# Another order of TensorE's and ScalarE's calls in the first half of a two-stage transformer kernel

## The reference

```
q, k, v = out @ Wq + bq, out @ Wk + bk, out @ Wv + bv       # 16 heads of 16
Qf, Kf  = favor(q), favor(k)      # exp(u - h), exp(-u - h), u = xs @ omega, h = 0.5 sum(xs*xs)
S_t     = S_(t-1) + Kf_t (x) v_t ;  z_t = z_(t-1) + Kf_t    # causal, per head
a_t     = (Qf_t . S_t) / (Qf_t . z_t + 1e-6)
h       = layer_norm(out + a @ Wo + bo)
out     = layer_norm(h + relu(h @ W1 + bf1) @ W2 + bf2)     # W1 256 x 1024
```

## Time and profile before

| | us |
|---|---|
| median of three runs | 2773.57 (2766.88 to 2775.44) |
| the profiled execution | 2769.28 |
| its span | 2767.5 |
| TensorE busy | 2633.1 (95%) |
| VectorE busy | 2308.6 (83%) |
| ScalarE busy | 1513.2 (55%) |
| GpSimd busy | 1455.6 (53%) |
| matmuls of key sums, rounds 0 to 23: first and last start | 48.6, 1334.8 |

### The profile page before, as it was taken

One profiled execution on the slowest core, in us unless ns is written; L12 is line 12 of the kernel. 1 busy time (PEld: TensorE's weight loads), 2 busy tenths in 40 slices (PEclk: granted clock), 3 DMA queues, 4 the chain that ended last, 5 costly groups with the idle time before them and its releaser, 6 DMA issues.

```text
span 2767.5 us, 61567 instructions
## 1 busy us (share of the span) xinstructions
PE 2633.1 (95%) x21416; PEld 2152.8 (78%) x21416; DVE 2308.6 (83%) x5242; ACT 1513.2 (55%) x3109; POOL 1455.6 (53%) x1406
## 2 busy tenths in 40 slices
PE   7799999999999999999888899999999999999997
PEld 4588887888788878777676688888878778788876
DVE  5788888888888898988898888888888888888875
ACT  3454455445544554444335766767766666666661
POOL 2343344344433444444466766665666666776653
PEclk8999999999999999999999999999999999999999
DMA  3100000010000010000111100000110100101001
GB/s 101 28 9 9 17 2 16 9 38 2 1 1 13 11 39 9 17 17 24 45 48 45 32 10 17 14 17 14 32 29 24 36 16 29 32 29 32 17 26 43
DMA packets 77731, 65.63 MB, mean 24 GB/s; under 512 B 15394, under 2 KB 72698, under 8 KB 77434
## 3 DMA queue, kind: packets, MB, share of 16 engines
q1 hardware_dynamic: 77434, 61.70, 7.5%
HBM read 49.10 MB, written 12.58 MB: 22 GB/s over the span
## 4 chain that ended last, share of the span: by engine, by line
PE 72%; DVE 11%; issue 7%; POOL 6%; ACT 2%; DMA 1%; SPq 0%; DVEq 0%; ACTq 0%; POOLq 0%
PE PS L273 64%; PE PS L813 3%; DVE Z L1532 2%; DVE U L1678 2%; POOL ZC L2356 1%; PE PS L766 1%; PE PS L775 1%; POOL RL L2316 1%; POOL X0L L2320 1%; PE PS L486 1%; PE PS L424 1%; PE PS L843 1%; DVE X L1532 1%; DVE PX L1532 1%; DVE PS L1915 1%
## 5 line engine op out<-in xcount | busy, mean ns | idle before, releaser
L1335 ACT ACTIVATE PR<-PS,SM 128x256 f32<-128x256 f32 (+1 forms) x512 | 279.2, 554 | 103.4 <-DVE SM L1920 101.8
L1133 ACT ACTIVATE FB<-PS,BC 128x512 f32<-128x512 f32 x192 | 132.1, 688 | 347.2 <-PE PS L273 344.0
L1678 DVE TENSOR_TENSOR U<-PS,CST 128x512 f32<-128x512 f32 x384 | 236.7, 677 | 33.5 <-PE PS L273 33.4
L1915 DVE CUSTOM_DVE_ANT_0 PS<-PS,MSK 128x256 f32<-128x256 f32 (+1 forms) x512 | 202.6, 436 | 48.8 <-PE PS L273 47.5
L2316 POOL TENSOR_TENSOR RL<-FB,RH 128x512 fp32r<-128x512 f32 x96 | 131.6, 1371 | 204.3 <-DVE RH L1656 204.3
L2328 POOL TENSOR_TENSOR SBD<-SBD,TMP 128x256 f32<-128x256 f32 x84 | 65.2, 776 | 317.6 <-DVE TMP L1670 317.6
L273 PE MATMUL PS<-W2H,RH 128*128 128x256 f32 x768 | 227.6, 296 | 0.3 <-DVE RL L1659 0.3
L2451 POOL TENSOR_TENSOR SM<-SM,COL 128x8 f32<-128x8 f32 x128 | 215.2, 1682 | 10.6
L273 PE MATMUL PS<-W2H,RL 128*128 128x256 f32 x768 | 215.8, 281 | 0.0
L273 PE MATMUL PS<-W2L,RH 128*128 128x256 f32 x768 | 215.7, 281 | 0.0
L273 PE MATMUL PS<-X1H,W1H 128*128 128x512 f32 x384 | 159.3, 415 | 8.5 <-ACT FB L1133 6.6
(11 more groups left out here) (264 smaller groups left out, 8914.1 us busy)
## 6 DMA issues: line engine op xcount, KB each, us to landing
PX<-in_L_attn_x SPq DMA_DIRECT2D x16, 512.0 KB, 4.0
TB<-in_k_rot SPq DMA_DIRECT2D x64, 128.0 KB, 2.1
SG<-in_L_attn_W SPq DMA_DIRECT2D x24, 256.0 KB, 2.8
xp_scratch<-PX SPq DMA_DIRECT2D x8, 512.0 KB, 3.0
xs_scratch<-X SPq DMA_DIRECT2D x64, 64.0 KB, 1.5
ZS<-xs_scratch SPq DMA_DIRECT2D x16, 256.0 KB, 2.9
GG<-xp_scratch SPq DMA_DIRECT2D x7, 512.0 KB, 3.7
out<-GG SPq DMA_DIRECT2D x7, 512.0 KB, 4.2
```

The lines of the kernel that those rows point to most:

```text
L1133: e.activation(FB[:, hb % 2, :], PS[:, 5, :], ACT.Relu, bias=BC[:, l % 2, 4 + hb:5 + hb]).then_inc(*a_re.up(n, hb))
L1335: t = e.activation(PR[:, par, 256 * i + lo:256 * i + hi], PS[:, 3 + par, 256 * i + lo:256 * i + hi], ACT.Exp, bias=S[:, 40 + 2 * g + i:41 ...
L1678: e.tensor_tensor(heads(U[:, u % 6, :], 4), heads(PS[:, g, :], 4), bcast(CM, 4), ALU.mult).then_inc(*d_mk.up(n, u))
L1915: t = e.tensor_tensor_reduce(o, o, MSK[:, z:z + hi - lo], 1.0, NEG, ALU.add, ALU.max, S[:, 32 + 2 * g + i:33 + 2 * g + i])
```

## The change

TensorE's list of rounds 2 to 23: `up(m, 2)` goes from behind `proj(n, 0)` to behind `down(m, 0)`; `values(n, 0)` stands in front of `down(m, 0)` and `values(n, 1)` behind `down(m, 1)`; `scores(n, 0)` goes in front of `key_sums(n)`; `up(m, 6)` in front of `down(m, 3)`; `down(m, 4)` in front of `up(m, 7)`; `down(m, 6)` in front of `turn_x(n + 1)`. ScalarE's list: both `attention` casts and `relu(m, 2)` in front of the features, `relu(m, 3)` behind all of them, `numerators(n, 1)` in front of `relu(m, 7)`, `numerators(n, 2)` behind `high_row`. In the second half ScalarE's waits for the end of the first half and for the bias transfers stand in front of the first `gelu` (tile 8) instead of at tiles 4 and 8. VectorE's, GpSimd's and SyncE's lists stay.

```diff
@@ tensor, for n in range(2, 24)
             up(m, 1)
             proj(n, 0)
-            up(m, 2)
             proj(n, 1)
             proj(n, 2)
             proj(n, 3)
+            values(n, 0)
             down(m, 0)
-            values(n, 0)
+            up(m, 2)
+            down(m, 1)
             values(n, 1)
-            down(m, 1)
             favor(n, 0, 2)
...
             up(m, 4)
+            scores(n, 0)
             key_sums(n)
-            scores(n, 0)
             down(m, 2)
             up(m, 5)
             sums(n, 0)
             scores(n, 1)
+            up(m, 6)
             down(m, 3)
-            up(m, 6)
             sums(n, 1)
             scores(n, 2)
+            down(m, 4)
             up(m, 7)
-            down(m, 4)
             sums(n, 2)
             scores(n, 3)
             down(m, 5)
             turn_h(w)
+            down(m, 6)
             if n < 23: turn_x(n + 1)
-            down(m, 6)
             if n < 23: up(w, 0)
@@ scalar, for n in range(2, 24)
             attention(w, 0)
+            attention(w, 1)
+            relu(m, 2)
             features(n, 0, 2)
-            relu(m, 2)
-            attention(w, 1)
             features(n, 1, 3)
             features(n, 2, 0)
+            features(n, 3, 1)
             relu(m, 3)
-            features(n, 3, 1)
             keep_rows(n, 0)
...
             relu(m, 6)
+            numerators(n, 1)
             relu(m, 7)
-            numerators(n, 1)
             high_mid(w, 0)
             high_mid(w, 1)
-            numerators(n, 2)
             if n < 23: high_row(n + 1, 0)
             if n < 23: high_row(n + 1, 1)
+            numerators(n, 2)
@@ scalar, gelu(q, hb)
             e.wait_ge(*f_ga[hb].at(q))
+            if q == 0 and hb == 0:
+                e.wait_ge(*t_bf.at(7))
+                first_half_over(e)
@@ scalar, second half's loop
-            if u == 4:
-                e.wait_ge(*t_bf.at(7))
...
-            if u == 8:
-                first_half_over(e)
```

## The result

| | before | after |
|---|---|---|
| median, runs | 2769.85 (2764.32 to 2775.44), 10 | 2778.83 (2775.85 to 2785.81), 10 |
| profiled execution, span | 2769.28, 2767.5 | 2784.48, 2782.7 |
| TensorE, VectorE busy | 2633.1, 2308.6 | 2641.6, 2305.7 |

The ratio is 1.0035, with a 95% interval of 1.0023 to 1.0048: 9.7 us slower (6.4 to 13.3). The forecast was +9.1. As a time, 2782.5, it lies 3.7 above the measured median: it was laid on 2773.57, the median of three runs of the kernel before, where ten runs give 2769.85.

The account below looks back on a forecast made before the run. TensorE, busy 977 of 990 us, was taken as the bound, its waits being all there is to win. Terms +5.0 + 0.6 + 1.0 + 2.5 made +9.1 us on the median 2773.57, stated as 2782.5; eight-in-ten range 2769 to 2792.

Parts of the forecast that it names:

- Scores and key sums: Late relu 3 makes VectorE's block 3 cast meet GpSimd's RL, delaying the scores: +0.28 in 18 rounds, 0.6 in round 20.
- The upper bound of +1.5: Worst case per round for scores and key sums, if VectorE's subtraction lets both ZC products go first.
- TensorE's edit alone: Scores in front of key sums with nothing to wait for would let down begin 0.22 earlier per round.
- Masks: Later VectorE chain makes sums(n, 0) wait some 0.2 for masks where a batch half begins (five rounds): +1.0.
- The split of the turns: down(m, 6) between turn_h and turn_x costs 0.12 for one more change of kind in 21 rounds: +2.5.
- Its later end moves high_row and lower. Covered: turn_x's later end moves high_row and lower(n + 1) by 1.0 to 1.4, without cost to TensorE.
- attention(w, 1) is early, so attn_out gets slack: ScalarE's second attention cast comes earlier, giving attn_out slack; listed among the edits at nothing.
- Rival 1: Ports are no obstacle: cast and subtraction end at 757.7, add_wo in time; -1.0, 2772.5 us; chance 0.28.
- Rival 2: The 1.0 behind the masks in sums(n, 2) goes if VectorE does norm1_b earlier; 2754 us; chance 0.06.
- Rival 3: Subtraction waits for both ZC products, or delayed chain misses sums(n, 1): +1.25 in 19 rounds, 2806 us; chance 0.10.

Follow-up runs that it names:

- e1: Changed kernel with relu(m, 3) put back in front of features(n, 3) on ScalarE; measured +4.1 us against the kernel before.
- e5: Changed kernel with GpSimd's RL of block 2 and ZC products cut to 16 of 512 columns; -1.1 us against the kernel before.
- e8: Kernel before with relu(m, 3) behind features(n, 3) and GpSimd's block 2 RL and ZC products on 16 of 512 columns; -5.0 us against before.
- e3: Kernel before with only relu(m, 3) moved behind features(n, 3) on ScalarE; +23.0 us against the kernel before.
- e2: Kernel before with only scores(n, 0) moved in front of key_sums(n) on TensorE; -1.4 us against the kernel before.
- e4: Changed kernel with down(m, 6) behind turn_x(n + 1) again, so the turns stand together; +17.7 us against the kernel before.
- c1: Changed kernel run a second time, unedited; +14.1 us against the kernel before, ratio 1.0051.
- e7: Kernel before with ScalarE's whole features part ordered as in the changed kernel, TensorE's order kept; +8.9 us against the kernel before.
- g1: Kernel before with scores(n, 0) in front of key_sums(n) and masks(n, 2) in front of norm1_b(w); -22.1 us against the kernel before.
- e6: Changed kernel with masks(n, 2) in front of norm1_b(w) on VectorE; -5.5 us against the kernel before.

## Why the prediction came out right, and where it did not

- **Scores and key sums, +0.28 in 18 rounds and 0.6 in round 20: right.** Cast 0.7 (0.58), subtraction 1.67 (1.65), wait 0.4 to 0.5 (9.6 in 19), pair +0.31. e1, e5 and e8 show the cause. Over rounds 2 to 20 the pair costs 5.3 in either trace of the changed kernel, where 5.6 was forecast. I had overlooked rounds 10 and 18, in which the key sums waited 0.6 for ZC before; there the pair became 0.1 to 0.2 shorter. And the 0.6 of round 20 came in the first trace alone. It all hung on a reckoning that put the cast 0.45 inside RL; it was 0.29. e3 shows how thin that is: RL 0.2 earlier and relu 3 0.3 later against `up(m, 4)`, and the price is 1.0. The upper bound of +1.5 was no fancy. I then wrote e3's expectation without redoing that reckoning, and missed by 15 us or more.
- **TensorE's edit alone, -0.22: right** (e2: 760.35 - 758.38, where the last matmul of `up` starts, makes 1.97 for the 2.24 of before: -0.27).
- **Masks, +1.0: too small (0.34 in five rounds, 1.7), cause incomplete.** I put it on add_wo's lateness. e1 and e2 have add_wo early and the same 0.34: the normaliser waits for the key sums behind the scores. e3 has the key sums first and add_wo late, and loses there too. In the changed kernel both come within 0.1 of each other, so either alone is enough.
- **The split of the turns, +2.5: mis-sized.** The prediction took 0.12 for one more change of kind. turn_x's group lasts 794.88 - 794.08 = 0.80, against 0.79; turn_h's 0.82 with `down` behind it, where 783.10 - 782.20 made 0.90. Together they are no longer than before (1.62 and 1.69), so the term is 0 in place of 2.5.
- **"Its later end moves high_row and lower. Covered": failed.** In rounds 3, 5 and 6 VectorE has the prologue's or the weights' work behind `lower`, so state(n, 3), numerators(n, 3) and relu(m, 0) come late. Round 5, ScalarE after:
```profile
296.44 0.38 ACT L1141 COPY NUM<-PS 128x256 f32<-128x256 f32 x1 [3.62 <-DVE TMP L1669]
```
  `up(3, 1)` starts at 297.55, 0.45 behind a matmul whose neighbours stand 0.12 apart. With 0.25 in rounds 10 and 18 it makes 1.8, and e4 gets that back. I followed round 13 and transferred it.
- **"attention(w, 1) is early, so attn_out gets slack": not free.** VP of round 20 is waited for 1.0 more. VectorE before, and after:
```profile
1135.94 4.57 DVE L1532 SCALAR_TENSOR_TENSOR PX<-Z,ST,PX 128x256 f32<-128x256 f32 x4
```
```profile
1147.85 5.58 DVE L1531 SCALAR_TENSOR_TENSOR PX<-Z,ST,PX 128x256 f32<-128x256 f32 x4
```
  GpSimd after, in that time:
```profile
1147.43 2.90 POOL L2310 TENSOR_TENSOR X<-X,BB 128x512 f32<-128x512 f32 x2
1150.35 2.80 POOL L2319 TENSOR_TENSOR X0L<-NUM,X0H 128x512 fp32r<-128x512 f32 x2
```
  Before, the second X0L product started at 1140.50, behind the norm; the earlier cast of ScalarE brought it inside. A fourth tile met a product: 1.0. The runs bear it out: every kernel with that cast early (changed, c1, e1, e4 to e7) waits 2.86 to 2.88 there, and before, e2, e3, e8 and g1 wait 1.85 to 1.87.
- **The clock: a cost that the prediction didn't name.** Behind the waits for VP TensorE ran at half clock for longer than before (last section): 2.8 us more in the first trace, which costs 1.4, and 2.1 more in c1, which costs 1.0.
- **The sum.** Of the pair's 5.3 the stretch, which starts at the key sums of round 2, holds 5.0. 5.0 + 1.7 + 0 + 1.8 + 1.0 + 1.4 = 10.9, near the stretch's +11.8; for c1 it is 10.5 of 11.2. The forecast of 9.1 was low by two or three, and as near as that by luck: the split's 2.5, which weren't there, stood for some 5 us that it left out.

Rival 1 would have been right without the overlap (e5: -1.1 for its -1.0). Rival 2's place was real and its condition as stated: the 1.0 in sums(n, 2) went only when VectorE's order changed (e6). Rival 3 didn't come in the changed kernel. e3 came nearest to it: there the cast itself fell into a ZC product.

What stays open: what makes the 12 us spread ahead of round 2; why the medians of e1, e3 and e4 stand 3.5 to 7 above their stretches (for e3 the short wait in front of round 23 may be 4 of it); and the 0.7 to 0.9 that the sum leaves.

## What to carry to other kernels

Before an activation or a cast is moved, write down which instruction of GpSimd runs when VectorE's next cast, or its next instruction with two SBUF operands, is asked for, in every kind of round and not in one. Here a late input cost little by itself; one that fell into a product cost the product's rest, and the next instruction one product more. And look for norms or other long groups in front of what a stalled matmul waits for: swapping two lines there was worth more (15.6 in the stretch) than this change cost.

## What the runs showed of the hardware

- When both engines have work queued, they take turns, one instruction each: a subtraction of 0.69 takes 1.65, a norm tile of 0.47 takes 1.4, and GpSimd's products grow only from 1.3 to 1.4 or 1.5. A cast of 0.42 takes up to 1.33.
- A wait can cost more than its length, and the same wait not always. Behind every wait of 4.3 us for VP TensorE's clock was granted at half, the 1.2 GHz level, for 3 to 6 us; behind those of 1.5 to 1.9 it stayed full. Behind 2.86 to 2.88 both occurred: it stayed full in the first trace of the changed kernel, e1, e4 and e5, and fell in c1, e6 and e7. After, round 20 and then round 21:
```profile
1154.24 1.08 PE L273 MATMUL PS<-U,OM 128*64 128x512 f32 x4 [2.88 <-DVE VP L1687]
...
1214.66 1.98 PE L273 MATMUL PS<-U,OM 128*64 128x512 f32 x4 [4.31 <-DVE VP L1687]
```
  and the granted clock behind the latter (the third number from the end, 0.50):
```profile
1216.00:1217.00 1.00, 1.00 (x4) 0.27 (x2) 1.00 (x2) 0.32 (x1) 0.00 (x0) 0.50 0.32 110
```
  c1, the same kernel, in its round 20, with the clock behind it:
```profile
1151.82 1.08 PE L273 MATMUL PS<-U,OM 128*64 128x512 f32 x4 [2.86 <-DVE VP L1687]
```
```profile
1153.00:1154.00 1.00, 1.00 (x4) 0.00 (x0) 1.00 (x2) 1.00 (x2) 0.00 (x0) 0.50 0.47 164
```
